# Third layer of a four-layer image network on Trainium2: the 64-row products of an image moved behind that image's 128-row products, with a signal and an eviction per image

## What is computed

```python
def _L2_conv_ref(x, weight):            # weight (32, 32, 5, 5)
    xp = jnp.pad(x, ((0, 0), (0, 0), (p, p), (p, p)), mode='reflect')   # p = 2
    ...                                 # the product of spectra: a circular convolution with the 5 x 5 kernel
    return out[:, :, p:-p, p:-p]
...
x = x + _L2_conv_ref(_gn(x), L2_conv_weight)
x = x + _L3_conv_ref(_gn(x), L3_conv_weights)
```

## Time and profile before

| what | value |
|---|---|
| three runs | 951.16, 938.11, 948.6 us, median 948.6 |
| the profiled execution | 947.15 us, of which 945.3 us from first to last instruction |
| TensorE busy | 775.2 us, 82% of the span |
| VectorE busy | 620.4 us, 66% |
| ScalarE busy | 480.7 us, 51% |
| granted TensorE clock, mean | 0.923 of full speed |
| `l2_stage` on TensorE | first product at 463.76 us, last one starts at 630.29 us |

### The profile page before, as it was taken

One profiled execution on the slowest core, in us unless ns is written; L12 is line 12 of the kernel. 1 busy time (PEld: TensorE's weight loads), 2 busy tenths in 40 slices (PEclk: granted clock), 3 DMA queues, 4 the chain that ended last, 5 costly groups with the idle time before them and its releaser, 6 DMA issues. The chain is left out here.

```text
span 945.3 us, 28083 instructions
## 1 busy us (share of the span) xinstructions
PE 775.2 (82%) x11423; PEld 647.9 (69%) x11423; DVE 620.4 (66%) x1144; ACT 480.7 (51%) x800; POOL 108.9 (12%) x96
## 2 busy tenths in 40 slices
PE   7999996874699464887599999966888489889997
PEld 7999995764588342766444444435777488889997
DVE  3455445778476697689687776775666677756453
ACT  0133336864434270754579997005887557764200
POOL 0000000110100162456003223000000100000000
PEclk9999998997699797899799999997999888999985
DMA  8599968750000100000000000004000448840054
GB/s 314 199 316 383 314 200 213 184 117 4 2 0 0 41 1 0 2 0 0 1 1 1 1 1 1 1 1 107 1 0 0 89 91 176 180 89 1 1 206 155
DMA packets 48380, 80.25 MB, mean 85 GB/s; under 512 B 19874, under 2 KB 38312, under 8 KB 43448
## 3 DMA queue, kind: packets, MB, share of 16 engines
q1 hardware_dynamic: 31672, 62.49, 23.8%
q10 hardware_dynamic: 16640, 16.78, 5.2%
HBM read 50.74 MB, written 27.92 MB: 83 GB/s over the span
## 5 line engine op out<-in xcount | busy, mean ns | idle before, releaser
L1618 DVE SCALAR_TENSOR_TENSOR X<-bank,c_power,X 32x512 f32 x128 | 96.7, 756 | 36.5 <-PE bank L1568 32.9
L1761 PE MATMUL bank<-m_xp,m_kf 128*32 128x64 f32 x2048 | 81.4, 245 | 22.2 <-DVE m_xp L1696 11.1
L1761 PEld LDWEIGHTS bank<-m_xp,m_kf 128*32 128x32 f32 x2048 | 80.3, 171 | 23.4 <-issue 23.3
L415 DVE COPY ks_rows<-bank 128x512 f32<-128x512 f32 x64 | 41.3, 687 | 67.3 <-PE bank L345 67.3
L215 DVE BATCH_NORM_STATS2 bn<-X 128x6 f32 x128 | 83.0, 683 | 2.9 <-POOL X L1358 1.6
L433 ACT COPY ks_spec<-bank 128x512 f32<-128x512 f32 x64 | 34.3, 589 | 98.8 <-PE bank L360 96.1
L1524 ACT ACTIVATE c_r<-X,c_nrm 32x1024 f32 (+1 forms) x56 | 75.0, 1340 | 2.4 <-DVE c_nrm L1592 1.1
L345 PE MATMUL bank<-ks_fw,ks_src 64*128 64x64 f32 x1024 | 68.7, 298 | 6.3 <-DMA ks_src<-in_L_conv_weights 6.3
L360 PE MATMUL bank<-ks_fh,ks_rows 64*128 64x128 f32 (+1 forms) x1152 | 72.5, 281 | 0.2 <-ACT ks_spec L433 0.2
L345 PEld LDWEIGHTS bank<-ks_fw,ks_src 64*128 64x128 f32 x1024 | 68.1, 215 | 6.2 <-issue 6.2
L360 PEld LDWEIGHTS bank<-ks_fh,ks_rows 64*128 64x128 f32 (+1 forms) x1152 | 67.6, 184 | 3.3 <-issue 1.8
(11 more groups left out here) (201 smaller groups left out, 1838.9 us busy)
## 6 DMA issues: line engine op xcount, KB each, us to landing
ks_src<-in_L_conv_weights SPq DMA_DIRECT2D x16, 1024.0 KB, 6.9
kf<-ks_spec ACTq DMA_DIRECT2D x16, 1024.0 KB, 8.9
m_kf<-kf SPq DMA_DIRECT2D x32, 512.0 KB, 8.4
X<-in_x SPq DMA_DIRECT2D x4, 2048.0 KB, 12.6
out_y<-X SPq DMA_DIRECT2D x32, 256.0 KB, 2.5
l_wb<-in_L_conv_weights_r SPq DMA_DIRECT2D x4, 512.0 KB, 11.1
l_wb<-in_L_conv_weights_i SPq DMA_DIRECT2D x4, 512.0 KB, 13.7
xf<-f_xm SPq DMA_DIRECT2D x16, 112.0 KB, 3.2
```

The costliest lines, as they stand in the source:

```text
L415: dve.tensor_copy(rows[p][:, m, :, C // 2 * g + r:C // 2 * (g + 1):2], ps[2 * g + r][:].rearrange("p (c n) -> p n c", n=N)).then_inc(rows_ ...
L1618: dve.scalar_tensor_tensor(x, of.rearrange("p (y x) -> p y x", x=HN), filt.power[at, 2:3], x, ALU.mult, ALU.add).then_inc(added, 1)
L1761: last = pe.matmul(ps[4 * half + m // 8][at:at + C, m % 8 * N:(m % 8 + 1) * N], kf[p][:, j, :, H * half + m], xp[half][:, j, m].rearrange( ...
```

## The change

The loop over the terms of the 64-row products moves into the loop over the images of the pair, so that an image has its 36 products of 128 rows, then its 18 of 64 rows. `conv` is raised once per image, and VectorE waits for it once per image, ahead of that image's four pieces. The number of products, loads, evictions and their shapes is unchanged.

```diff
@@ -1576,14 +1576,13 @@
                                     for oy in range(2):
                                         ky = 1 if step_y == 0 else 2 - 2 * oy
                                         product(odd, oy, ky, kx, t, slice(0, P), i == 0 and step_y == 0, False)
-                        for i, (kx, t) in enumerate(terms):
-                            for odd in range(2):
+                            for i, (kx, t) in enumerate(terms):
                                 for oy in range(2):
 
                                     first = 2 * C * ((oy + odd) % 2)
                                     m = product(odd, oy, 2 * oy, kx, t, slice(first, first + 2 * C), False,
                                                 i == len(terms) - 1)
-                        m.then_inc(conv, 1)
+                            m.then_inc(conv, 1)
@@ -1607,8 +1606,9 @@
-                        dve.wait_ge(conv, TILES // 2 * q + n + 1)
                         for odd, oy, ox in np.ndindex(2, 2, 2):
+                            if (oy, ox) == (0, 0):
+                                dve.wait_ge(conv, TILES * q + 2 * n + odd + 1)
```

## The result

The changed kernel takes 969.37 us (median of 6 runs, 967.4 to 982.6) and the kernel before 946.58 us (median of 6, 938.11 to 951.16): 1.0251 times as long, with a 95% interval of 1.0193 to 1.0309. It is slower by some 24 us by the ratio and by 22.8 us between the medians; the forecast was 27.9 us of cost, 976.5 us against a median of 948.6, with a range of 966 to 985.

A forecast was written before the change was run, and what follows sets the result against it. TensorE's stream was taken to bound the stage, with VectorE having slack. 31.0 us more on TensorE less 3.1 saved at the end gave +27.9, forecast as 976.5 us against a median of 948.6, range 966 to 985.

The forecast's parts named there:

- The bound: Stage of the change: TensorE busy in all of a 40.60 us group, VectorE in 29.9; TensorE's stream sets its length.
- The slot: 64-row blocks: two products take a slot as long as four, about 0.22 us; a second block costs 2.18 us per step.
- The first two steps: Stage's start, where TensorE waits for VectorE's parts: step 0 costs nothing, step 1 costs 0.5 us instead of 2.18.
- the sum on TensorE: TensorE's stage: 0.5 us plus 30.5 for the other 14 steps, so its last product ends 31.0 us later.
- The last step: Stage's end: only four evictions left behind TensorE's last product, saving 3.1 us; TensorE's pause goes from 10.52 to 7.4.
- The sum: Whole kernel: + 31.0 - 3.1 = +27.9 us, forecast as 976.5 us against the median of 948.6.
- The first: 64-row blocks: instructions, not columns, pace a slot; slots of two take 0.11 us, kernel not slower, 947.3 us; chance 4%.
- The second: 64-row blocks: each term pays an uncovered load of 0.105 us, 30 us in all, to some 1006 us; chance 3%.
- the third: 64-row blocks: half clock with half the array empty, 2.0 us longer each, 64 us, to 1040 us; chance 2%.
- The fourth: 64-row blocks partly overlap neighbouring 128-row terms, or pair slots come nearer 0.15 us: some 958 us; chance 4%.

The follow-up runs named there:

- e1: Kernel before with the changed kernel's TensorE order, but one signal and one VectorE wait per pair as before: 975.24 us against 943.87, 1.0363.
- e2: Kernel before with TensorE's order kept, but a signal and a VectorE wait per image: 944.44 us against 943.87, 1.0034.
- e6: Against the kernel before: both images' alternating 64-row products placed between their 128-row products, signals and evictions per image: 938.61 us against 943.69, 0.9951.
- e4: Kernel before with the odd images' 64-row products left out, output incomplete: 949.44 us against 943.87, 1.0047.
- e3: Kernel before with the 64-row block's loops exchanged: the even image's 18 products, then the odd image's, in one block: 961.30 us against 943.87, 1.0198.
- e5: The changed kernel again, unaltered, beside the kernel before, for more runs and a second profile: 969.27 us against 943.69, 1.0304.
- e8: Kernel before with the images alternating by three terms in the 64-row block: 943.84 us against 943.69, 0.9991.
- e7: Against the kernel before: e6's order in the last step, every second step elsewhere turned round so 64-row blocks meet: 941.16 us against 943.69, 0.9954.

## Why the prediction was right

**The bound.** "The stage lasts as long as TensorE's stream, plus what VectorE still has to do": shown by e1 and e2, of which the first carries the whole cost and the second none, and for what stands behind the last product by e6.

**The slot.** Eighteen slots for nine, 2.10 + 0.08 = 2.18 us a step: measured 12.38 - 10.16 = 2.22. e4 shows the ground for it by itself, two products in a slot of the same length.

**The first two steps and the sum on TensorE.** Predicted 31.0 us; 31.5 in e1, which has the clock of the kernel before in the stage. 14 steps by 0.04 us are the rest. In the changed kernel's own two profiles it is 32.8 and 32.9, the clock at the stage's start having fallen. The sum had no term for this; it was worth 1.4 us. That the change causes this was not shown, since it falls ahead of the first moved product and e3 and e6 show the same mean.

**The last step.** Predicted 3.1 us saved; 10.53 - 7.43 = 3.1, and the same in e6, where it stands alone. The forecast took the clock to fall in the shortened pause as in the long one, and layer four to begin as before, with 1.5 us either way. The clock did fall, sooner after the last product than before: that product ended at 665.77, and the clock was 1.00 in 667 to 668 and 0.56 in 668 to 669. The stretch from the statistics to the last stage took 257.10 us against 256.24.

**The sum.** 27.9 us predicted. 22.8 between medians in the first comparison, 25.6 in e5, and 24 and 29 by the ratios. Two profiled executions with nearly the same last stage of layer four, the one of the kernel before and e5's, differ by 30.0 us; two with different ones, 47.86 and 36.80 us, by 21.8. That last stage was not in the sum. Its length differs from execution to execution of one program (36.8 and 46.6 us in the changed kernel; 36 to 52 over all ten profiles), by a third of the effect and more. That the medians differ from the sum for the same reason is likely and not shown, since they have no profiles.

The time itself, 969.37 us, lies 7.1 us under the likeliest value of 976.5. 5.1 of them are the smaller difference of medians, and 2.0 are the median of before, 948.6 over three runs and 946.58 over six. The forecast had left 4 us on the low side for its own terms and the rest, down to 966, for the scatter of runs. The stage's own terms came out above the sum (by 0.5 us, and by 1.4 more with the clock), not below it, so what brought the time to the low side stands outside the sum, in parts of the kernel for which the forecast had only the width of its range. The stage bears out the mechanism; that the whole time came out near is no further proof of it.

**The rivals.** The first (a slot paced by its instructions) is refuted by e4. The second (loads no longer hidden) and the third (half clock in the blocks) would show in the timeline of the changed kernel, which has slots of 0.21 to 0.24 us and a granted clock of 1.00 from 518 to 567.6. The fourth, 64-row blocks that overlap with their neighbours or pair slots near 0.15 us, gave "nothing but that no row shows a pair of 64-row f16 products alone" as its ground. The blocks of 2.10 us in the changed kernel rule it out there, but e3 and e8 show an overlap that the forecast hadn't thought of: TensorE does fill quarters out of order. That it didn't help the changed kernel because 36 products of 128 rows stand between an image's block and the next is my reading; no run varied what stands between. The Trainium skill's rule that was weighed there ("TensorE: Matmul & The Clock Gate", section "Packing small matmuls: row/col tiling", loads overlap only across row groups) is not borne out: slots of 64-row products in the same two quarters run at 0.22 us with their loads hidden. The section itself also names a load into the background weight buffer as a second way, and no run here separates the two. The same section says that matmuls start in strict program order; e3 and e8 contradict it, and had my sum needed an adjacent block, it would have been wrong by 0.85 us a step, as e3's expectation was.

## What to carry to other kernels

Products that fill only part of the array are worth what stands beside them: before they are moved, look at which quarter each uses and whether their start times in the timeline coincide, and keep partners together when their consumers are split. A result can be had earlier by reordering whole blocks around the shared one (e6) instead of cutting the shared one in two; but an early signal is worth only the consumer's work behind the last product, here 3 us once, while the cut cost 2.2 us in each of 14 steps. Read an effect of a few per cent in the stages that it touches, when another stage of the same program varies by 10 us; and before a sum is held against a whole time, look at how far the stages outside the sum differ between two profiles.

## What the runs showed of the hardware

TensorE started 64 x 64 products whose quarter was free ahead of four to six products that stood before them in the program and waited for theirs (e3: the 19th of a block at 501.86, the 13th to 18th from 502.08 to 502.51; e8: the 7th at 497.66, the 3rd at 497.88).

Changing from 128-row to 64-row products and back cost 0.19 us in all, read from the start times of the earlier trace rows, and 0.21 by e7's seams.

A slot of 64-row products lasted the same 0.21 to 0.24 us with two products in it as with four (a block of nine 2.10 us in e4 and in the changed kernel, as before).

The granted clock fell to the lower level in layer four's last stage of the kernel before, with TensorE busy for most or all of each stretch around the fall, and stayed there to the end (0.50 from 925 to 945.3, with TensorE busy for 13.9 of these 20.3 us):

```profile
910.00:915.00 5.00, 4.25 (x152) 4.11 (x152) 3.20 (x6) 0.00 (x0) 0.00 (x0) 1.00 0.76 279
915.00:920.00 5.00, 5.00 (x120) 5.00 (x116) 1.82 (x4) 0.00 (x0) 0.00 (x0) 0.60 0.47 171
920.00:925.00 5.00, 5.00 (x100) 5.00 (x100) 0.98 (x2) 0.00 (x0) 0.00 (x0) 0.50 0.56 210
```

TensorE was busy for 4.25 of 5 us ahead of the fall, with one pause of 0.75 us, and for all of the ten after it, with 100 products in 5 us where 152 had been. In the changed kernel's profile the same stage had 1.00 from 930.3 to 965. What decides it was not tried.
